# An LSTM recommender on one core: 14 of 28 layer-1 cells by seven block products instead of eight

## The reference

```
rp   = concat(region_tbl[region_idx], poi_tbl[poi_idx])
nv   = concat(rp @ W_rp + b_rp, coords @ W_co + b_co)
conv = elu(conv1d(nv, conv_w, width 3) + conv_b)               # 8 steps x 32
emb  = tanh(concat(car_tbl[car], week_tbl[week], time_tbl[time]))  # 27
x    = concat(conv, emb at each step)                          # 8 x 59
step: g = xt @ Wih.T + h @ Whh.T + bias; i, f, gg, o = split(g, 4)
      c = sigmoid(f) * c + sigmoid(i) * tanh(gg); h = sigmoid(o) * tanh(c)
y = ((h_last @ W1 + b1) @ W2 + b2) @ W3 + b3
```

## Time and profile before

| what | us |
|---|---|
| median of 3 runs | 1076.36 (1075.54 to 1076.51) |
| the profiled execution | 1084.42 |
| its span, first to last instruction | 1082.6 |
| PE busy | 1062.0 |
| DVE busy | 724.6 |
| ACT busy | 517.2 |
| POOL busy | 318.4 |

### The profile page before, as it was taken

The page is one execution under the profiler, slowest core; times in us unless marked ns, Lnnn a source line. Parts: engine busy times, 40 slices in busy tenths (PEclk is TensorE's granted clock), DMA queues, the critical chain, the costliest instruction groups (busy, mean ns, idle before and its releaser), DMA issues.

```text
span 1082.6 us, 14274 instructions
## 1 busy us (share of the span) xinstructions
PE 1062.0 (98%) x4905; PEld 509.7 (47%) x4905; DVE 724.6 (67%) x1155; ACT 517.2 (48%) x757; POOL 318.4 (29%) x353
## 2 busy tenths in 40 slices
PE   8699999999999999999999999999999999999998
PEld 6444444444445444444445444444444544444445
DVE  5489966666767866556867865567676775666554
ACT  3466444444555544434564544345554544444433
POOL 7650055524430055542440035552450000000000
PEclk9799999999999999999999999999999999999999
DMA  9310100000101100000010010000010110000001
GB/s 264 74 19 9 31 3 3 2 1 2 31 2 40 25 10 2 2 2 1 5 29 36 5 33 2 3 2 2 2 32 1 40 30 1 1 0 1 1 1 39
DMA packets 32082, 21.26 MB, mean 20 GB/s; under 512 B 19629, under 2 KB 25865, under 8 KB 32019
## 3 DMA queue, kind: packets, MB, share of 16 engines
q1 hardware_dynamic: 21223, 19.25, 6.2%
q0 software_dynamic: 9984, 1.12, 2.9%
q10 hardware_dynamic: 812, 0.07, 0.1%
HBM read 9.92 MB, written 4.19 MB: 13 GB/s over the span
## 4 chain that ended last, share of the span: by engine, by line
PE 96%; issue 1%; DVE 1%; ACT 1%; another core or an unknown queue 0%; DVEq 0%; ACTq 0%; POOL 0%; POOLq 0%
PE acc L1547 53%; PE acc L1538 29%; PE acc L1532 5%; PE aux L1774 2%; PE acc L1361 2%; PE aux L1449 1%; PE acc L1605 1%; PE acc L1614 1%; PE aux L1482 1%; PE aux L1374 0%; PE aux L1663 0%; PE aux L1488 0%; PE aux L1462 0%; ACT gates L849 0%; PE aux L1622 0%
## 5 line engine op out<-in xcount | busy, mean ns | idle before, releaser
L1547 PE MATMUL acc<-h_part,wh 128*128 128x512 f16 (+1 forms) x2640 | 644.2, 380 | 0.0
L1547 PEld LDWEIGHTS acc<-h_part,wh 128*128 128x128 f16 x2640 | 240.3, 98 | 314.6 <-issue 55.4
L1538 PE MATMUL acc<-h_part,wh 128*128 128x512 f16 (+1 forms) x1440 | 346.8, 379 | 0.5 <-DVE gates L1160 0.5
L849 ACT ACTIVATE gates<-acc,gate_bias,unscale 128x512 f32<-128x512 f32 x246 | 189.5, 777 | 305.1 <-PE acc L1547 261.8
L849 ACT ACTIVATE gates<-gates,gate_bias,unscale 128x512 f32<-128x512 f32 x242 | 190.1, 811 | 143.9 <-DVE gates L1160 129.2
L1538 PEld LDWEIGHTS acc<-h_part,wh 128*128 128x128 f16 x1440 | 139.9, 98 | 171.8 <-issue 6.8
L666 POOL DMA_INDIRECT feat<-in_L_rec_region_tbl,region_idx x160 | 158.8, 993 | 170.6 <-PE acc L1547 129.8
L1160 DVE TENSOR_TENSOR gates<-acc,emb_gates 128x512 f32<-128x512 f32 x239 | 160.3, 687 | 51.1 <-PE acc L1547 45.2
L666 POOL DMA_INDIRECT feat<-in_L_rec_poi_tbl,poi_idx x120 | 115.5, 963 | 109.1 <-PE acc L1547 89.6
L1532 PE MATMUL acc<-x_in,wx 96*128 96x512 f32 (+1 forms) x239 | 133.6, 565 | 0.3 <-issue 0.2
L1207 DVE TENSOR_TENSOR h_full<-gates,tanh_c 128x512 f32<-128x512 f32 x120 | 82.6, 688 | 73.6 <-ACT tanh_c L856 70.1
(11 more groups left out here) (185 smaller groups left out, 428.0 us busy)
## 6 DMA issues: line engine op xcount, KB each, us to landing
out<-y SPq DMA_DIRECT2D x16, 256.0 KB, 2.1
x_in<-conv_hi SPq DMA_DIRECT2D x56, 64.0 KB, 2.0
feat<-in_L_rec_region_tbl,region_idx POOLq DMA_INDIRECT x160
w<-in_L_rec_W SPq DMA_DIRECT2D x4, 512.0 KB, 5.2
w_nat<-in_L_rec_Whh SPq DMA_DIRECT2D x2, 1024.0 KB, 9.6
w<-in_L_rec_W SPq DMA_DIRECT2D x1, 2048.0 KB
feat<-in_L_rec_poi_tbl,poi_idx POOLq DMA_INDIRECT x120
x_in<-conv_lo SPq DMA_DIRECT2D x28, 64.0 KB, 2.0
```

The costliest lines, as they stand in the source:

```text
L849: nc.scalar.activation(gates[layer][:, j, g, :], source, ACT.Tanh if g == GATE_G else ACT.Sigmoid, bias=gate_bias[:, layer, m:m + 1], scal ...
L1538: mm = nc.tensor.matmul(bank, wh[:, 1, a, c, rows], h_part[0][:, s.write_slot, b, c, :], start=(c == 0 and a == b == HI), stop=(s.first an ...
L1547: mm = nc.tensor.matmul(bank, wh[:, own_w, a, c, rows], h_part[layer][:, s.read_slot, b, c, :], start=False, stop=(c == HK - 1 and a == LO))
```

## The change

A layer-1 cell computes two 2 x 2 block products (layer 0's h and its own h): the blocks of the weights are (output half j) x (contraction half c), those of h are (contraction half c) x (left and right 256 samples). In 14 cells (t = 4, 5 of batch 0; t = 2 to 5 of the others) the eight block products are replaced by seven with sums of blocks (Winograd's form). Both layers' products go into the same banks, for a pair of gates at a time: 14 products of 12 matmuls of 256 columns. Four sums of weight blocks for each layer (`w_form`, float16 high and low) are made once by DVE in the cells t = 2, 3 of batch 0, between the operations of those cells (`weight_forms`, `cell_with_forms`). Four sums of h blocks (`t_full`, split in `t_part0` and `t_part1`) are made for each step by DVE (`t_forms`, `t_low`) and ACT (`put_t_hi`).

Two results that share a partial sum are had by copying a bank: ACT copies from PSUM to PSUM or to SBUF (`part_copy`), PE goes on accumulating in the banks, and DVE adds SBUF and PSUM parts (`part_sums`). So the gates of such a cell come in quarters of 128 x 256. Its last quarters, c and h (the "tail") are worked on in the next layer-0 cell. In these stages ("lower", "upper", "rest") the element-wise operations take both halves at once, 1024 columns, and ACT makes the high part of h. tanh(c) now overwrites the gate I, so `tanh_c` is gone. Batch 0 is written out before the loop over batches, which has two rounds now. The weights' scale has 2^12 in place of 2^14, in layer 1 one scale for both halves j of a gate (one more small DVE operation in the opening). GpSimd's gathers wait for the same counts of `gate_act` instead of `gate_acc`. The buffers `t_part0`, `t_part1`, `t_full` share memory with `h_last` and `y`, hence the wait for `y_free` in a layer-0 cell.

```diff
 def body(n, following):
+        for t in range(FIRST7, first_fast):
+            yield "cell", s0
+            yield "cell", before
+        low = lower(first_fast + 1, None, before)
+        yield low
+        yield "upper", first, low[1]
+        if first_fast == FIRST7:
+            with eng.Fori(0, steps - 6) as u:
...
+                yield "lower", s0, tail, None
+                yield "upper", s1, s0
+        low = lower(last_t - 1, fast(last_t - 3))
+        yield low
         if following:
             yield "turn", n + 1, 0
             yield "turn_emb", n + 1
+        end = fast(last_t - 2)
+        yield "upper", end, low[1]
+        low = lower(last_t, end)
+        yield low
+        yield "rest", low[1]
 # POOL
-                            pool.wait_ge(gate_acc[at[0]], at[1])
+                            pool.wait_ge(gate_act[at[0]], at[1])
 # ACT
+            def lower_acts(s, tail, plain_tail):
+                if tail is not None:
+                    act.wait_ge(part_sum, sums + 4)
+                    quarter(tail, 0, GATE_F, RIGHT, gates[1][:, 0, GATE_F, RIGHT], count=True)
+                    act.wait_ge(part_acc, steps + 14)
+                    quarter(tail, 1, GATE_F, LEFT, half_bank(A2, 0), count=True)
...
+                gate_act0(s, 0, GATE_I)
+                if tail is not None:
+                    tanh_both(tail)
+                gate_act0(s, 0, GATE_G)
+                gate_act0(s, 0, GATE_F)
+                if tail is not None:
+                    put_h_hi(tail)
+                if forms.forms is not None:
+                    put_t_hi(forms)
+                gate_act0(s, 0, GATE_O)
+                for g in s.gates:
+                    gate_act0(s, 1, g)
+            def upper_acts(s, low):
+                act.wait_ge(h_done[1], ahead + s.half)
+                for bank, source, step in ((B1, A1, 1), (B2, A2, 2)):
+                    act.wait_ge(part_acc, steps + step)
+                    nc.scalar.copy(bank, source).then_inc(part_copy, 1)
+                for bank, pair, step in ((B1, (GATE_I, GATE_G), 3), (B2, (GATE_F, GATE_O), 4)):
+                    act.wait_ge(part_acc, steps + step)
+                    for a, g in enumerate(pair):
+                        quarter(s, 0, g, LEFT, half_bank(bank, a))
+                tanh_both(low)
...
+                put_h_hi(low)
...
+                act.wait_ge(part_sum, sums + 1)
...
 # DVE
+            def lower(s, tail, plain_tail):
+                if tail is not None:
+                    both_fc(tail)
+                    add_embeddings(s, *places[0])
+                    both_c(tail)
+                    add_embeddings(s, *places[1])
+                    add_embeddings(s, *places[2])
+                    both_h(tail)
+                    if tail.forms is not None:
+                        t_forms(tail)
+                    both_lo(tail)
+                    add_embeddings(s, *places[3])
+                    add_embeddings(s, *places[4])
+                    if tail.forms is not None:
+                        t_low(tail)
+                    for place in places[5:]:
+                        add_embeddings(s, *place)
+            def upper(s, low):
+                both_ig(low)
+                both_fc(low)
+                both_c(low)
+                both_h(low)
+                if low.forms is not None:
+                    t_forms(low)
+                both_lo(low)
+                part_sums(s, 0)
+                if low.forms is not None:
+                    t_low(low)
+                for k in range(1, ADDS7):
+                    part_sums(s, k)
+                both_ig(s)
+            def t_forms(s):
+                nc.vector.tensor_tensor(t_full[:, 0:2, :], h4[:, 1:4:2, :], h4[:, 0:2, :], ALU.subtract
...
+                nc.vector.tensor_tensor(t_full[:, 2, :], h4[:, 3, :], t_full[:, 0, :], ALU.subtract
...
+                nc.vector.tensor_tensor(t_full[:, 3, :], h4[:, 2, :], t_full[:, 2, :], ALU.subtract
 # PE
+                product(A1, FIRST_PAIR, A11, B11, True, 1)
+                product(A2, SECOND_PAIR, A11, B11, True)
+                pe.wait_ge(part_copy, copies + 1)
+                product(B1, FIRST_PAIR, A12, B21, False, 1)
+                pe.wait_ge(part_copy, copies + 2)
+                product(B2, SECOND_PAIR, A12, B21, False)
+                pe.wait_ge(gate_sum, low.tile + 7)
+                pe.wait_ge(t_done[0], s.fast + 1)
+                pe.wait_ge(t_done[1], s.fast + 1)
+                pe.wait_ge(forms_ready, 2 * FORMS)
+                product(E1, FIRST_PAIR, S1, T1, True, 1)
+                product(A1, FIRST_PAIR, S2, T2, False)
+                pe.wait_ge(gate_sum, low.tile + 8)
+                product(E2, SECOND_PAIR, S1, T1, True, 1)
+                pe.wait_ge(part_copy, copies + 3)
+                product(E1, FIRST_PAIR, S4, B22, False)
+                product(A2, SECOND_PAIR, S2, T2, False, 1)
+                pe.wait_ge(part_copy, copies + 4)
+                product(A1, FIRST_PAIR, S3, T3, False)
+                pe.wait_ge(part_copy, copies + 6)
+                product(A2, SECOND_PAIR, S3, T3, False, 1)
+                pe.wait_ge(part_sum, sums + 2)
+                product(A1, FIRST_PAIR, A22, T4, False)
+                pe.wait_ge(part_copy, copies + 5)
+                product(E2, SECOND_PAIR, S4, B22, False, 2)
+                pe.wait_ge(part_sum, sums + 3)
+                product(A2, SECOND_PAIR, A22, T4, False)
```

More of the change, by code:

```diff
@@ new lines, in tanh_both, with put_h_hi @@
+            def tanh_both(s):
+                layer = s.layer
+                act.wait_ge(c_done[layer], s.half + HK)
+                nc.scalar.activation(gates[layer][:, :, GATE_I, :], cell_c[layer][:, :, :], ACT.Tanh
+                                     ).then_inc(tanh_c_done[layer], HK)
+            def put_h_hi(s):
+                layer = s.layer
+                act.wait_ge(h_full_done[layer], s.split + HK)
+                nc.scalar.copy(h_part[layer][:, s.write_slot, HI, :, :], h_full[:, :, :]
+                               ).then_inc(h_hi_done[layer], HK)
@@ L932, in _ @@
                     elu_parts(chunk_of(*stage[1:]), slice(0, NCOL))
+                elif kind == "lower":
+                    lower_acts(*stage[1:])
+                elif kind == "upper":
+                    upper_acts(*stage[1:])
+                elif kind == "rest":
+                    tanh_both(stage[1])
+                    put_h_hi(stage[1])
                 elif kind == "cell":
@@ new lines, in lower @@
+            def lower(s, tail, plain_tail):
+                places = [(j, g) for j in range(HK) for g in s.gates]
+                if tail is not None:
[14 more added lines that the diff above has]
+                        add_embeddings(s, *place)
+                else:
+                    for place in places[0:3]:
+                        add_embeddings(s, *place)
+                    t_forms(plain_tail)
+                    add_embeddings(s, *places[3])
+                    t_low(plain_tail)
+                    for place in places[4:]:
+                        add_embeddings(s, *place)
@@ new lines, in part_sums @@
+            def part_sums(s, k):
+                steps, copies = s.fast * STEPS7, s.fast * COPIES7
+                step, copy, j, pair, bank = ((8, 4, 0, PAIR_A, E1), (10, 3, 1, PAIR_A, A1), (11, 5, 1, PAIR_B, A2),
+                                             (13, 6, 0, PAIR_B, E2))[k]
+                dve.wait_ge(part_acc, steps + step)
+                dve.wait_ge(part_copy, copies + copy)
+                out = gates[1][:, j, pair, RIGHT]
+                nc.vector.tensor_tensor(out, gate_pair(bank), out, ALU.add).then_inc(part_sum, 1)
@@ new lines, in upper, with rest @@
+            def upper(s, low):
[7 more added lines that the diff above has]
+                part_sums(s, 0)
+                if low.forms is not None:
+                    t_low(low)
+                for k in range(1, ADDS7):
+                    part_sums(s, k)
+                both_ig(s)
+            def rest(s):
+                both_ig(s)
+                both_fc(s)
+                both_c(s)
+                both_h(s)
+                both_lo(s)
@@ L1346, in _ @@
                     elu(chunk_of(n, c), slice(0, NCOL), (c, slice(0, NCOL)), free)
+                elif kind == "lower":
+                    lower(*stage[1:])
+                elif kind == "upper":
+                    upper(*stage[1:])
+                elif kind == "rest":
+                    rest(stage[1])
+                elif kind == "cell" and stage[1].fill is not None:
+                    cell_with_forms(stage[1])
                 elif kind == "cell":
@@ L1557, in opening_cell, with after_fast @@
+            def after_fast(tail, place):
+                if place < 2:
+                    pe.wait_ge(gate_act[1], tail.tile + 1)
+                else:
+                    pe.wait_ge(part_sum, tail.fast * ADDS7 + (1, 4)[place - 2])
```

329 lines of the change are left out of this document (293 added, 36 removed).

## The result

On the chip of the first comparison the change made the kernel faster: 1048.26 us (1047.64 to 1048.95) beside 1076.11 for the kernel before, ratio 0.974 (0.973 to 0.976). That is 27.9 us, where 20.6 were forecast. One execution of r10 (1195.29 us, at a granted clock of 0.848) was in a slower state and is left out of its figures.

The account below looks back on a forecast made before the run. TensorE, busy 98%, was taken as the bound; -33.2 + 6.0 + 1.8 + 3.8 + 0.5 + 0.7 + 0.2 - 0.4 = -20.6 us from 1076.4 gave 1055.8 us, 8-in-10 range 1047 to 1071.

Parts of the forecast that it names:

- Minus 33.2 for the matmuls: PE in 14 layer-1 cells: fewer matmul columns save 2.37 us per cell, 33.2 us in all, if PE never waits.
- The first bank copy, 6.0 + 1.8 + 0.4: PE's third product waits for ACT's copy: 10 x 0.6 us, 3 x 0.6 behind transposes, 0.4 in batch 0.
- 0.12 us taken for each dependent DVE operation: DVE chain: an operation needing the previous result was taken to start 0.12 us after its end.
- Behind the transposes: Three batches: the transposes' copy and two embedding tanhs stand before the first bank copy, 3 x 0.6 = 1.8 us lost.
- Batch 0's weight sums, 3.1 at the fifth tile: DVE's weight sums in two batch 0 cells delay the fifth layer-0 tile: 0.3 us lost, then 3.1.
- Batch end, 0.5: ACT does tanh and h copy before the ELU, reaching the next cell's first gate later: 0.5 us for all three.
- Register work, set-up and the outer edge, 0.5 lost together: PE loop counters 0.7 us, setup and batch 0's longer code 0.2, one taken outer-loop edge fewer minus 0.4.
- 2-page window: Inner body of 448 loads and matmuls might miss instruction fetch: three edges stall, sum 1.2 us longer or more.
- Part sum 1 "just fits", 0.3 spare: Fast cell: part_sum 1 is done at 26.93 us, PE asks at 27.29 before the twelfth product; 0.3 us spare.
- the rival built on it: Part sums set the step: delay of part_sum 1 beyond 0.3 us stalls the twelfth product; 1090 us, chance 0.08.
- GpSimd's pace, "no loss": Gathers paced by gate activations come in bursts but land in time: no loss, unless landing took over 5 us.

Follow-up runs that it names:

- r10: Changed kernel with gathers paced by TensorE's tiles, first bank copy before the last gate activation, one batch 0 weight form moved later: 1071.80 us, 0.985 of the kernel before.
- r2: Changed kernel with ACT's first bank copy moved ahead of the layer-0 cell's last gate activation: 1111.39 us, 1.022 of the kernel before.
- r4: Changed kernel with one extra 512-column DVE add before `t_low` in ten layer-0 cells: 1.028 of the kernel before; batch 3 cells 18.26, then 19.08 us.
- r6: Changed kernel with one extra 512-column DVE add between first part sum and `t_low` in ten fast cells: 1.031 of the kernel before.
- r1: The changed kernel run again unchanged, on another chip than the first comparison: 1114.74 us, 1.027 of the kernel before.
- r3: Changed kernel with gathers paced by TensorE's tile counts (`gate_acc`) again, as in the kernel before: 1074.63 us, 0.991 of the kernel before.
- r9: Changed kernel without the gathers of region and poi rows for batches 1 to 3: 1059.55 us, 0.975 of the kernel before.
- r11: Changed kernel with gathers paced by TensorE's tiles, but released eight at a time: 1148.00 us, 1.059 of the kernel before.
- r12: r10 with each gather of batches 1 to 3 also waiting until the one before has landed: 1320.33 us, 1.215 of the kernel before.

## Why the prediction was right in one place and wrong in another

On the first chip, point by point:

- *Minus 33.2 for the matmuls*: right. An unstalled step takes 30.67 us instead of 33.04, and 14 x 2.37 = 33.2. (Two slips cancel in it: 14 x 12 x 0.109 is 18.3, not 18.35, and the cell takes 18.26; but the layer-0 cell takes 12.41 instead of 12.32.)
- *The first bank copy, 6.0 + 1.8 + 0.4*: the mechanism is the one named, shown by r2 (gone) and r4 (0.60 for 0.60). **Its size is the mis-sized term**: 4.6 measured. Most of it came from the 0.12 us taken for each dependent DVE operation, where 0.03 to 0.05 stand in the trace; the third product starts 15.32 us after the first layer-0 tile instead of 15.55, and the first two end 0.1 later than worked out. Behind the transposes 0.5 us more is lost, where 0.6 was forecast.
- *Batch 0's weight sums, 3.1 at the fifth tile*: right place, a third of the size, 1.1 (13.58 us for that layer-0 cell instead of 12.51). Timeline of DVE and PE there:

```profile
188.31 0.68 DVE L1450 TENSOR_TENSOR tanh_part<-wh 128x512 f32<-128x512 f16 x1
189.02 0.70 DVE L1450 TENSOR_TENSOR tanh_part<-tanh_part,relu_part 128x512 f32<-128x512 f32 x1
...
194.14 1.88 DVE L1351 TENSOR_TENSOR gates<-acc,emb_gates 128x512 f32<-128x512 f32 x3
...
194.88 0.50 PE L1911 MATMUL acc<-x_in,wx 96*128 96x512 f32 x1 [0.80 <-DVE gates L1351]
```

  The sums are 0.71 apart, not 0.81: 12 x 0.71 + 4 x 0.46 = 10.4 instead of 11.9 us a cell. The 0.3 in the first of the two cells didn't appear.
- *Batch end, 0.5*: some 0.3 in the three. *Register work, set-up and the outer edge, 0.5 lost together*: 33.2 - 4.6 - 1.1 - 0.3 = 27.2, so these gave 0.6 instead. That is about what the missing taken edge of the batch loop gives: the step in which it stood takes 33.81 us instead of 34.41. The edge that is left starts its group 0.40 us late (at 620.67). The steps through the inner loops take 30.89 to 30.97 us, which is the 30.67 and the stall before the third product; so the inner edges cost nothing, and the stall that the prediction worked out from the Trainium skill's "2-page window" (Runtime: NRT & Kernel Launch, "Instruction fetch mechanics") did not come.
- *Part sum 1 "just fits", 0.3 spare*: right. r6 adds 0.60 and loses 0.14 to 0.17, so 0.43 to 0.46 are spare; the rival built on it had its place right and its condition was not met.

The errors are 3.6 us (8.2 forecast for the copies), 2.3 (3.4 for batch 0's sums) and 1.3 (1.0 for the rest): the 7.2 us between forecast and result. The first two have that one source in large part. In kind the forecast was right, and every loss in it came out smaller or equal.

- *GpSimd's pace, "no loss"*: right on the first chip, wrong on the chip of r1 and r3, where it costs 40 us, and r9 and r11 show the same effect on another. I had foreseen the bursts and priced only when rows land, not what a burst does to the engines beside it. The kernel before already showed such waits of ScalarE (63.7 us, of them 20.8 for late counts, 8.8 after the opening), which I passed over since that engine had time to spare. The change takes that spare away: its bank copies stand between TensorE's products.

What is shown: gathers are needed for the loss (r9), their runs decide its size (r3, r11), and keeping them apart takes the late counts away (r12). What passes from GpSimd to the others is shown in part: TensorE's semaphore updates come late, and its readers with them. What holds the updates up stays open. The trace lists 44 and 31 instruction packets in both r1 and the first chip's profile, and none is on record in the 3.77 us above; the packets of a gather take 0.3 to 0.4 us of its 3.1. The Trainium skill (Runtime: NRT & Kernel Launch, "Instruction fetch mechanics") says that each engine's sequencer fetches its next instructions over a DMA queue of its own while it executes, mostly hidden. The trace speaks against a late fetch here: TensorE issues its matmuls at full rate all through the stop, and ScalarE starts 0.02 us behind the update. Nor is it known why the first chip is free of it, with runs of up to 13 gathers; that it is the chip, and not something else that differed between the first comparison and the later runs, was not tested.

## What to carry to other kernels

When an edit moves *when* an engine works, price its bursts and not only its deadlines: spread GpSimd's gathers over counts that come evenly, and read the spare time of the engines beside it, since a schedule that uses this spare time is exposed to stalls that the old one absorbed. Waits on "remote" of an engine off the path are a warning for the day when it stands on it: look when the semaphore it waits for is updated, and when the instruction that counts it ended. Before you say that an engine is held, see whether it is the count that is late. Judge a change of a few per cent on more than one chip, and read a schedule's terms in a stretch that the disturbance doesn't touch.

## What was not expected of the hardware

- While gathers are issued back to back, 1.25 us apart, TensorE's semaphore updates come up to 4.05 us (r1) and 7.12 us (r11) after the matmul that gives them, instead of 0.014 us, while TensorE goes on issuing. ScalarE idled up to 7.95 us for one, VectorE up to 7.33 (both r11). Counts of ScalarE and VectorE weren't late in any trace. TensorE's longest "issue" wait in r11, 3.56 us, ends 0.06 us behind the ScalarE instruction that it needs, so it is held through its readers there. Late counts cost idle time in batches that gather on three chips (r1 to r11) and in the opening on all four, and in the first chip's trace nowhere.
- A gather of 128 rows takes 0.94 us on GpSimd. Its packets run from 1.6 to 2.0 us after the issue, and its semaphore is complete at 2.35 (medians of r12). The Trainium skill (DMA: Bandwidth & Descriptors, "Anatomy of one DMA — SWDGE (gpsimd) path") gives about 2.0 us fixed for such a transfer; the 2.35 here is somewhat more, and a GpSimd that waits for it starts the next gather 3.1 us after the last.
- Dependent DVE operations of 512 columns follow each other at 0.71 us, 0.03 after the end of the one before.
